# Softmax denominators of an audio-tower block: reciprocals on VectorE in place of a logarithm and an exponential on ScalarE

## The chip, the cores and the metric

The kernel runs on one core of one Trainium2 chip. The metric is the device time of one execution in microseconds (us); lower is better. The kernel before was run three times: 326.23, 329.70 and 332.12 us, median 329.7 us.

## What is computed

The input x has shape (8, 256, 128), float32. Three layers follow one another:

```python
h = tok(x)                      # gated recurrence, (8, 257, 128)
h = h + attn(layernorm(h))      # 8 heads of 16 features
h = h + ffn(layernorm(h))       # shared expert + 16 experts, top 2
```

The layer that matters here is the attention, cut to its core:

```python
scores = einsum('bnhd,bmhd->bhnm', q, k) / sqrt(128)
prob = softmax(scores, axis=-1)
out = einsum('bhnm,bmhd->bndh', prob, v)
```

Keys and values of batch row b come from the other half of the batch (row b+4 or b-4). The feed-forward layer computes all 16 experts and the shared one for every position and weighs them with the router's top two.

## The kernel before, in words

**Units.** The batch is worked off in four units u = 0 to 3 of two rows s = 0, 1 (rows u and u+4, so that each is the other's key and value side). Features lie on the 128 partitions, and the 257 positions, padded to 258 (`W`), lie along the free axis. Each unit passes three stages: T (recurrence, first layer norm, q, k, v), A (attention, second layer norm, routing) and F (13 chunks of 128 feed-forward features, `NF`). The units overlap: while unit u is in F, unit u+1 goes through T and A.

**Order.** A unit's work is cut into pieces with names (`unit_pieces`, L86 to L113), and `ENGINES` (L60) says which engines take part in each: P is TensorE, A ScalarE, V VectorE, G GpSimd, S SyncE. For each engine the table `AT` (L119 to L177) gives every piece of that engine its place; `order` (L195) sorts by it, and `run` (L367) issues the instructions in that order. So each engine works through a fixed list of its own, and semaphores (`S[name]`, waited for with `ge`) tie the lists together. `SLOT` (L180) says which of the four PSUM slots each use of PSUM takes.

**The end of a softmax.** For every (u, s) the product of the exponentiated scores and the values arrives in a PSUM slot ("pv"). The values carry columns of ones, so that numerators and denominators stand in the same slot, in alternating groups of 16 partitions. Then:

- `apart` (L639, ScalarE) copies one bank of the slot, masked, into `rden` (denominators, L645) and `nom` (numerators, L646), both 128x258.
- `join` (L806, VectorE) adds the other bank's half to `rden` (L810) and `nom` (L812), and gives the PSUM slot free.
- `rden_` (L648, ScalarE) takes the natural logarithm of `rden` (L651) and then the exponential of its negative (L653). Ahead of them stands `tables(SET_EXP_LN)`.
- `norm` (L814, VectorE) shuffles the reciprocals onto the numerators' partitions (`swapped`, L817), multiplies (L820) and adds `h1`, the output of the recurrence, into `h2n` (L822).

When both `norm` pieces of a unit are done, TensorE starts the second layer norm (`center`, L1009), whose result feeds the router and the experts. GpSimd's `h1` of the next unit (L474) also waits for the unit before's `h2n`. On ScalarE `keep` (L675) copies `h2n` to `h2`, which the feed-forward sums are added to.

**Tables.** `tables(number)` (L523) issues an activation table load (L527) only when the set differs from the one loaded last in ScalarE's list. Set 6 has the exponential and the logarithm; set 0 has the exponential and tanh. `variance`, `rden_` and pieces 1, 2 and 7 of `token` ask for set 6; `tanh` (L695), once for each of the 13 chunks of a unit, asks for set 0. The exponentials of the scores (`st_`, L627) ask for none.

**Feed-forward.** Chunk c of unit u: TensorE computes the gate and up halves (`half_`, L1145), ScalarE evicts the gate (L686), GpSimd clips it (L499), ScalarE takes tanh (L699), VectorE clips the up half (`clip_up`, L890), combines (`gated`, L896, and `gu`, L911), GpSimd multiplies by the routing weight (L510), TensorE applies the second weight in three bursts (`down`), which VectorE adds (`add`, L914).

Of the kernel before, what the change touches and what calls it, by code (L numbers as in the profile page):

```python
# [25 lines left out]
SET_EXP_LN = 6  # L26
# [10 lines left out]
for _name, _n in (("wtok", 3 * P), ("btok", 3), ("cmat", P), ("omat", P), ("wq", P), ("wk", P), ("wv", P),  # L37
# [48 lines left out]
def unit_pieces(u):  # L86
# [11 lines left out]
    for s in range(2):  # L98
        parts = [(c, i) for c in range(2) for i in range(2)]
        a += [("A", "scores", u, s, *x) for x in parts] + [("A", "max", u, s, *x, h) for x in parts for h in range(2)]  # L100
        a += [("A", n, u, s) for n in ("mlast", "mtop", "plast")]
        a += [("A", "keys", u, s, *x) for x in parts] + [("A", "st", u, s, *x, h) for x in parts for h in range(2)]
        a += [("A", "pvl", u, s)]
        a += [("A", "pv", u, s, c) for c in range(2)] + [("A", n, u, s) for n in ("apart", "join", "rden", "norm")]
# [3 lines left out]
    for c in range(NF):  # L108
# [25 lines left out]
    ),  # L134
# [13 lines left out]
    ),  # L148
# [15 lines left out]
    ),  # L164
# [6 lines left out]
    ),  # L171
    "S": (
        0, 3, 4, 5, 6, 7, 8, 9, 10, 11, 13, 12, 14, 15, 16, 31, 1, 17, 18, 20, 19, 21, 22, 23, 25, 24, 28, 29, 27, 26,
        30, 41, 2, 32, 33, 36, 35, 34, 37, 38, 39, 40, 42, 43, 45, 44, 46, 55, 47, 48, 49, 50, 51, 52, 53, 54, 57, 56,
        59, 58, 61, 60, 62,
# [57 lines left out]
def build(nc, x_in, consts_in, w1_in, w2_in, spill, out):  # L233
    ctx = ExitStack()
    with ctx:
# [282 lines left out]
        def _(act):  # L518
# [129 lines left out]
            def rden_(st, u, s):  # L648
                tables(SET_EXP_LN)
                ge(act, "join", 2 * u + s + 1)  # L650
                a(rden[:, :], rden[:, :], ACT.Ln).then_inc(S["lden"], 1)  # L651
                ge(act, "lden", 2 * u + s + 1)
                a(rden[:, :], rden[:, :], ACT.Exp, scale=-1.0).then_inc(S["rden"], 1)  # L653
# [607 lines left out]
```

## Time and profile before

| | us |
|---|---|
| three runs | 326.23, 329.70, 332.12 (median 329.7) |
| the profiled execution's own time | 330.53 |
| span of the profiled execution, first to last instruction | 328.8 |
| mean granted clock of TensorE, as a share of full speed | 0.957 |

The profiled execution took 330.53 us, of which 1.7 us lie outside the span. Windows and start times in the rows count from the start of the span. "Busy" is time in which an engine executes instructions; waits are not in it.

### The profile page before, as it was taken

Reading aid. Unit: us, or ns where it says so; the run is one execution under the profiler, and the core shown is the slowest. Engines: PE = TensorE matmul, PEld = TensorE weight load, DVE = VectorE, ACT = ScalarE, POOL = GpSimd, SP = SyncE. Lnnn points to the kernel's source line nnn. Section 1 sums busy time; section 2 is a strip of 40 time slices with the busy share of each in tenths; the row PEclk is TensorE's granted clock in tenths of the full one; section 3 lists DMA queues with packets and bytes.
Section 4 is the critical chain, followed back from the end, with each engine's and each line's share of the span. In section 5 each row is a group of like instructions: output and inputs, shape, how many; then the busy total and the mean of one; then the engine's idle time right before and its main releaser. Section 6 shows DMA issues by size and latency. Waiting matters only on the chain.

```text
span 328.8 us, 6060 instructions
## 1 busy us (share of the span) xinstructions
PE 292.7 (89%) x2056; PEld 225.7 (69%) x2056; DVE 261.1 (79%) x488; ACT 237.4 (72%) x406; POOL 159.2 (48%) x138
## 2 busy tenths in 40 slices
PE   7467899968899999999989999999999979997973
PEld 5236665446587777876847968979778769986751
DVE  2397693425999999998899989788989789998870
ACT  3978905859689878799989989777877855754121
POOL 2002830010827857552856864711485643487960
PEclk9879999989999999999999999999999999999585
DMA  6500100000004304100131204100432200064211
GB/s 248 209 8 0 35 1 2 2 0 32 0 6 146 111 5 102 37 2 0 53 89 60 67 0 128 35 9 8 163 104 61 89 7 8 21 179 133 64 40 32
DMA packets 11318, 18.87 MB, mean 57 GB/s; under 512 B 1868, under 2 KB 4052, under 8 KB 11160
## 3 DMA queue, kind: packets, MB, share of 16 engines
q1 hardware_dynamic: 11288, 18.49, 18.1%
q8 instruction: 17, 0.28, 0.3%
q14 instruction: 13, 0.11, 0.1%
HBM read 17.03 MB, written 1.19 MB: 55 GB/s over the span
## 4 chain that ended last, share of the span: by engine, by line
PE 55%; DVE 17%; ACT 13%; issue 7%; POOL 3%; DMA 2%; POOLq 1%; SPq 0%; ACTq 0%; DVEq 0%
PE slot L988 54%; DVE mx L792 3%; DVE ubuf L890 2%; ACT L527 2%; DVE tbuf L911 1%; DMA cst<-in_consts 1%; ACT zabs L539 1%; ACT pt L637 1%; ACT soft L540 1%; DVE h2n L822 1%; DMA cwb<-spill 1%; POOL te L510 1%; PE slot L1186 1%; POOL soft L448 1%; ACT zlog L546 1%
## 5 line engine op out<-in xcount | busy, mean ns | idle before, releaser
L510 POOL TENSOR_TENSOR te<-tbuf,cwb 128x516 f32<-128x516 f32 x48 | 70.9, 1486 | 36.3 <-DVE tbuf L911 31.6
L988 PE MATMUL slot<-xh,w1h 128*128 128x258 f32 x208 | 65.2, 314 | 3.4 <-ACT gbuf L686 0.7
L499 POOL TENSOR_SCALAR gbuf<-gbuf,fpar 128x516 f32<-128x516 f32 x52 | 48.4, 934 | 38.5 <-ACT gbuf L686 38.2
L988 PE MATMUL slot<-xh,w1l 128*128 128x258 f32 x208 | 58.7, 282 | 0.0
L988 PE MATMUL slot<-xl,w1h 128*128 128x258 f32 x208 | 58.7, 282 | 0.0
L988 PE MATMUL slot<-te,w 128*128 128x258 f32 x208 | 52.8, 409 | 4.6 <-POOL te L510 2.4
L988 PEld LDWEIGHTS slot<-te,w 128*128 128x128 f32 x208 | 41.8, 205 | 12.7 <-POOL te L510 3.2
L896 DVE SCALAR_TENSOR_TENSOR tbuf<-tbuf,gbuf 128x516 f32<-128x516 f32 x52 | 46.8, 907 | 3.9 <-ACT tbuf L699 3.8
L988 PEld LDWEIGHTS slot<-xh,w1h 128*128 128x128 f32 x208 | 39.3, 189 | 13.6 <-issue 12.5
L686 ACT ACTIVATE gbuf<-slot,cst 128x516 f32<-128x516 f32 x52 | 35.1, 688 | 18.3 <-PE slot L988 14.8
L699 ACT ACTIVATE tbuf<-gbuf,fpar 128x516 f32<-128x516 f32 x52 | 36.9, 723 | 11.7 <-POOL gbuf L499 8.0
L792 DVE TENSOR_REDUCE mx<-slot 128x2 f32<-128x514 f32 x64 | 40.9, 685 | 2.6 <-PE slot L988 2.4
L890 DVE TENSOR_SCALAR ubuf<-slot,fpar 128x516 f32<-128x516 f32 x48 | 38.2, 806 | 5.5 <-PE slot L988 5.4
L911 DVE SCALAR_TENSOR_TENSOR tbuf<-ubuf,fpar,tbuf 128x516 f32<-128x516 f32 x48 | 39.6, 838 | 0.5
L988 PEld LDWEIGHTS slot<-xl,w1h 128*128 128x128 f32 x208 | 39.5, 190 | 0.6 <-issue 0.2
L637 ACT ACTIVATE pt<-slot 128x516 f32<-128x516 f32 x64 | 34.7, 602 | 7.1 <-PE slot L988 6.8
L988 PEld LDWEIGHTS slot<-xh,w1l 128*128 128x128 f32 x208 | 39.2, 189 | 0.0
L448 POOL TENSOR_TENSOR soft<-soft,zlog 128x1024 f32<-128x1024 f32 x3 | 7.1, 2356 | 48.0 <-ACT zlog L546 48.0
L988 PE MATMUL slot<-ka,qa 32*128 32x258 f32 x256 | 27.1, 425 | 3.1 <-DVE mx L792 1.3
L527 ACT ACT_TABLE_LOAD x22 | 28.2, 1283 | 1.1 <-PEq L1253 0.7
L988 PE MATMUL slot<-qa,ka 32*128 32x258 f32 x256 | 24.8, 420 | 1.2 <-DVE qa L804 0.5
L988 PEld LDWEIGHTS slot<-ka,qa 32*128 32x128 f32 x256 | 14.5, 183 | 11.2 <-DVE mx L792 3.7
(155 smaller groups left out, 482.5 us busy)
## 6 DMA issues: line engine op xcount, KB each, us to landing
cwb<-spill SPq DMA_DIRECT2D x32, 193.5 KB, 2.9
cwb<-spill SPq DMA_DIRECT2D x32, 129.0 KB, 3.0
cwb<-spill SPq DMA_DIRECT2D x32, 64.5 KB, 2.8
pt<-in_w SPq DMA_DIRECT2D x1, 1664.0 KB, 9.0
xt<-in_x SPq DMA_DIRECT2D x4, 256.0 KB, 3.8
out<-osb SPq DMA_DIRECT2D x8, 128.0 KB
w<-in_w SPq DMA_DIRECT2D x1, 832.0 KB, 10.5
cst<-in_consts SPq DMA_DIRECT2D x1, 528.5 KB, 5.4
```

The source lines that it names most:

```text
L448: e.tensor_tensor(soft[:, :, :, :], soft[:, :, :, :], zlog[:, 0:2, :, :], ALU.add).then_inc(S["sp"], 1)
L499: g.tensor_scalar(gbuf[:, p, :, :], gbuf[:, p, :, :], fpar[:, GHI, c:c + 1], fpar[:, GLO, c:c + 1], ALU.min, ALU.max).then_inc(S["gclip"], 1)
L510: g.tensor_tensor(te[:, c % NTE, :, :], tbuf[:, c % NB, :, :], cwb[:, c % NSP, :, :], ALU.mult)\
L527: nc.scalar.add_instruction(mybir.InstLoadActFuncSet(name=nc.get_next_instruction_name(), act_func_set_id=number, ins=[], outs=[]))
L637: release(a(pt[:, c, 4 * h + i:4 * h + i + 3:2, :], scores, ACT.Exp, scale=SCORE_SCALE), st, name)
L686: release(a(gbuf[:, c % NB, :, :], slot(st, ("g", c))[:, :, 0:W], ACT.Identity, bias=par[:, B1G, c:c + 1]), st, ("g", c))
L699: a(tbuf[:, c % NB, :, :], gbuf[:, c % NB, :, :], ACT.Tanh, scale=fpar[:, HA, c:c + 1])\
L792: release(v.tensor_reduce(tops, slot(st, name)[:, :, 0:N], AX_X, ALU.max), st, name)
L890: release(v.tensor_scalar(ubuf[:, p, :, :], slot(st, ("u", c))[:, :, 0:W], hi, lo, ALU.min, ALU.max), st, ("u", c))
L896: v.scalar_tensor_tensor(tbuf[:, p, :, :], tbuf[:, p, :, :], 1.0, gbuf[:, p, :, :], ALU.add, ALU.mult)\
L911: v.scalar_tensor_tensor(tbuf[:, p, :, :], ubuf[:, p, :, :], fpar[:, UB, c:c + 1], tbuf[:, p, :, :], ALU.add, ALU.mult).then_inc(S["gu"], 1)
L988: return nc.tensor.matmul(out_, lhsT, rhs, start=start, stop=stop, **k)
```

## The change

- The piece `rden` is gone from the piece lists, from `ENGINES` and from ScalarE's table of functions, with its table request, its logarithm, its exponential and the semaphore `lden`.
- `norm` on VectorE now waits for `join` itself and issues `v.reciprocal` on `rden` in place, 128x258 float32. The shuffle waits for it.
- `norm` has one more wait, for `h2` at u, ahead of the addition that writes `h2n`: in the kernel before, the copy `keep` of the unit before stood ahead of `rden_` in ScalarE's list, which ordered the two.
- All places in `AT` for the five engines, and the slots in `SLOT`, are new. They hold the same pieces otherwise. The lists differ from those of before mostly by swaps of neighbours and moves over a few places.

```diff
@@ ENGINES, unit_pieces
-    "apart": "A", "join": "V", "rden": "A", "norm": "V", "gate": "PV", ...
+    "apart": "A", "join": "V", "norm": "V", "gate": "PV", ...
-        a += [...] + [("A", n, u, s) for n in ("apart", "join", "rden", "norm")]
+        a += [...] + [("A", n, u, s) for n in ("apart", "join", "norm")]
@@ ScalarE
-            def rden_(st, u, s):
-                tables(SET_EXP_LN)
-                ge(act, "join", 2 * u + s + 1)
-                a(rden[:, :], rden[:, :], ACT.Ln).then_inc(S["lden"], 1)
-                ge(act, "lden", 2 * u + s + 1)
-                a(rden[:, :], rden[:, :], ACT.Exp, scale=-1.0).then_inc(S["rden"], 1)
@@ VectorE
             def norm(st, u, s):
                 n = 2 * u + s + 1
+                ge(dve, "join", n)
+                v.reciprocal(rden[:, :], rden[:, :]).then_inc(S["rden"], 1)
                 ge(dve, "rden", n)
                 v.stream_shuffle(swapped[:, :], rden[:, :], ...).then_inc(S["swap"], 1)
                 released(dve, st, ("pv", s))
                 ge(dve, "swap", n)
                 v.tensor_tensor(nom[:, :], nom[:, :], swapped[:, :], ALU.mult).then_inc(S["even"], 1)
                 ge(dve, "even", n)
+                ge(dve, "h2", u)
                 v.tensor_tensor(h2n[:, s, 0:N], nom[:, 0:N], h1[:, s, 0:N], ALU.add).then_inc(S["h2n"], 1)
```

What the new lists hold around the change, read off the tables of the diff: ScalarE's list asks for a table load 14 times, the first included, where the old one asks 22 times. Of the copies `keep`, that of unit 0 now stands ahead of `apart` of (1, 0); that of unit 1 stands behind it: after `apart` of (2, 0) come one gate eviction, one tanh, two score exponentials, one tanh, and then `keep` of unit 1. In VectorE's list `norm` of (2, 0) follows `join` of (2, 0) with one `clip_up` between them, and `gated` of chunk 4 comes behind it.

## Rows read from the trace of the kernel before

**Rows 1.** The page, busy time, share of the span and instruction counts by engine.

```profile
PE 292.7 (89%) x2056; PEld 225.7 (69%) x2056; DVE 261.1 (79%) x488; ACT 237.4 (72%) x406; POOL 159.2 (48%) x138
```

**Rows 2.** The page, the chain that ended last, shares of the span by engine.

```profile
PE 55%; DVE 17%; ACT 13%; issue 7%; POOL 3%; DMA 2%; POOLq 1%; SPq 0%; ACTq 0%; DVEq 0%
```

**Rows 3.** Busy time by stretch: window, its length, then the engines.

```profile
core 0: us, PE busy (x) PEld busy (x) DVE busy (x) ACT busy (x) POOL busy (x), PEclk, DMA share, GB/s
58.00:70.00 12.00, 10.58 (x90) 5.44 (x82) 5.53 (x14) 7.86 (x18) 1.27 (x1) 1.00 0.00 1
80.00:100.00 20.00, 18.31 (x139) 14.02 (x138) 19.66 (x45) 15.47 (x28) 9.21 (x8) 1.00 0.03 9
100.00:120.00 20.00, 19.59 (x166) 15.12 (x164) 19.27 (x33) 17.04 (x30) 16.51 (x14) 1.00 0.34 101
...
140.00:160.00 20.00, 19.36 (x126) 14.48 (x126) 17.48 (x44) 19.72 (x33) 9.19 (x8) 1.00 0.01 1
160.00:180.00 20.00, 18.48 (x169) 13.24 (x168) 19.96 (x34) 18.31 (x29) 13.36 (x12) 1.00 0.26 76
...
260.00:268.00 8.00, 6.46 (x65) 5.00 (x54) 7.18 (x14) 5.09 (x9) 3.24 (x4) 1.00 0.20 66
...
80.00:180.00 100.00, 95.30 (x735) 72.20 (x733) 95.03 (x179) 87.14 (x143) 60.61 (x49) 1.00 0.17 49
180.00:260.00 80.00, 78.71 (x613) 64.64 (x609) 68.47 (x131) 64.97 (x116) 45.45 (x39) 1.00 0.22 64
```

**Rows 4.** Groups of ScalarE by form: count, busy us, mean ns, idle before.

```profile
L699 ACT ACTIVATE tbuf<-gbuf,fpar 128x516 f32<-128x516 f32 x52 | 36.9, 723 | 11.7 <-POOL gbuf L499 8.0 <-POOL te L510 3.2 <-DVE te L907 0.3
...
L637 ACT ACTIVATE pt<-slot 128x516 f32<-128x516 f32 x64 | 34.7, 602 | 7.1 <-PE slot L988 6.8
L527 ACT ACT_TABLE_LOAD x22 | 28.2, 1283 | 1.1 <-PEq L1253 0.7
```

**Rows 5.** The tile rden: count, ns min/median/max, first and last start.

```profile
L651 ACT ACTIVATE rden<-rden x8: 418/420/468, 61.1 to 263.8; 128x258 f32<-128x258 f32 x8
L653 ACT ACTIVATE rden<-rden x8: 418/419/421, 61.6 to 264.2; 128x258 f32<-128x258 f32 x8
...
L817 DVE STREAM_SHUFFLE swapped<-rden x8: 437/444/452, 62.0 to 264.7; 128x258 f32<-128x258 f32 x8
```

**Rows 6.** The tile gm of the router, VectorE operations on 5 elements a partition.

```profile
L859 DVE TENSOR_TENSOR gm<-gm x4: 153/155/158, 82.2 to 277.8; 128x5 f32<-128x5 f32 x4
...
L866 DVE TENSOR_SCALAR gm<-gm x4: 158/165/1954, 83.4 to 279.0; 128x5 f32<-128x5 f32 x4
L868 DVE RECIPROCAL gm<-gm x4: 189/190/190, 85.4 to 279.1; 128x5 f32<-128x5 f32 x4
```

**Rows 7.** Timeline of VectorE, 58 to 70 us: start, us, what, idle before.

```profile
65.62 0.48 DVE L810 SCALAR_TENSOR_TENSOR rden<-slot,cst,rden 128x258 f32<-128x258 f32 x1 [2.15 <-ACT nom L646]
...
67.04 0.44 DVE L817 STREAM_SHUFFLE swapped<-rden 128x258 f32<-128x258 f32 x1
```

**Rows 8.** The chain that ended last, 110 to 116 us: start, us, what.

```profile
111.97 0.44 DVE swapped L817
```

**Rows 9.** Timeline of VectorE, 127 to 134 us.

```profile
129.07 0.47 DVE L810 SCALAR_TENSOR_TENSOR rden<-slot,cst,rden 128x258 f32<-128x258 f32 x1
...
129.86 0.80 DVE L890 TENSOR_SCALAR ubuf<-slot,fpar 128x516 f32<-128x516 f32 x1
131.13 0.01 DVE L817 LOAD_MASK_SELECT swapped<-rden  x1 [0.47 <-ACT rden L653]
```

**Rows 10.** Timeline of ScalarE, 127 to 134 us.

```profile
128.93 1.28 ACT L527 ACT_TABLE_LOAD   x1
130.22 0.42 ACT L651 ACTIVATE rden<-rden 128x258 f32<-128x258 f32 x1
```

**Rows 11.** Timeline of VectorE, 260 to 268 us.

```profile
262.49 0.48 DVE L810 SCALAR_TENSOR_TENSOR rden<-slot,cst,rden 128x258 f32<-128x258 f32 x1
...
264.68 0.01 DVE L817 LOAD_MASK_SELECT swapped<-rden  x1 [0.59 <-ACT rden L653]
```

More of the change, by code:

```diff
@@ L103, in unit_pieces @@
         a += [("A", "pvl", u, s)]
-        a += [("A", "pv", u, s, c) for c in range(2)] + [("A", n, u, s) for n in ("apart", "join", "rden", "norm")]
+        a += [("A", "pv", u, s, c) for c in range(2)] + [("A", n, u, s) for n in ("apart", "join", "norm")]
     a += [("A", n, u, 2) for n in ("center", "variance", "scale")] + [("A", "gate", u)]
@@ L120 @@
     "P": (
[13 rows of a table removed]
[13 rows of a table added]
     ),
     "A": (
[12 rows of a table removed]
[12 rows of a table added]
     ),
     "V": (
[14 rows of a table removed]
[14 rows of a table added]
     ),
     "G": (
[5 rows of a table removed]
[5 rows of a table added]
     ),
     "S": (
-        0, 3, 4, 5, 6, 7, 8, 9, 10, 11, 13, 12, 14, 15, 16, 31, 1, 17, 18, 20, 19, 21, 22, 23, 25, 24, 28, 29, 27, 26,
-        30, 41, 2, 32, 33, 36, 35, 34, 37, 38, 39, 40, 42, 43, 45, 44, 46, 55, 47, 48, 49, 50, 51, 52, 53, 54, 57, 56,
-        59, 58, 61, 60, 62,
+        0, 3, 4, 5, 7, 6, 10, 9, 8, 11, 12, 15, 13, 14, 16, 31, 1, 17, 18, 19, 20, 21, 22, 23, 24, 25, 27, 29, 26, 28,
+        30, 34, 2, 32, 33, 36, 38, 35, 37, 39, 40, 41, 42, 43, 45, 44, 46, 54, 47, 48, 49, 51, 50, 52, 53, 55, 56, 57,
+        58, 59, 60, 61, 62,
     ),
@@ L330, in build @@
                  "efin h1 sq1 sq2 rs1 rs2 vpad bq bk nm "
-                 "mxl pv apart join swap even lden rden h2n h2 xh xl cwl gtop gexp gclip uclip th gg gu shared te").split()
+                 "mxl pv apart join swap even rden h2n h2 xh xl cwl gtop gexp gclip uclip th gg gu shared te").split()
         S = {n: sem("r_" + n) for n in names}
@@ L727, in _ @@
             run("A", {"token": token, "center": center, "variance": variance, "q": q_, "k": k_, "v": v_, "weights": weights,
-                      "clamps": clamps, "plast": plast, "st": st_, "apart": apart, "rden": rden_, "split": split, "route": route,
+                      "clamps": clamps, "plast": plast, "st": st_, "apart": apart, "split": split, "route": route,
                       "cwt": cwt_, "keep": keep, "g": gate_half, "u": up_half, "tanh": tanh, "out": out_})
```

110 rows, old and new, of tables (AT, ENGINES, SLOT) are left out of this document.

## Prediction

> **What bounds the kernel now.** I read the page's busy times first. TensorE is busy for 292.7 of 328.8 us, VectorE for 261.1, ScalarE for 237.4, GpSimd for 159.2 [rows 1]. The chain of work that ended last gives 55% to TensorE, 17% to VectorE and 13% to ScalarE [rows 2]. So no engine holds the end alone, and the change takes work from the third engine and gives it to the second. What that is worth depends on the stretch, so the windows come next [rows 3]. Three kinds of stretch are to be seen there. From 58 to 70 us, at the end of unit 0's attention, no feed-forward work exists yet that could cover a late softmax: TensorE has 1.4 us of idle time in it, and VectorE and ScalarE have room. From 80 to 180 us TensorE (95.3 of 100) and VectorE (95.0 of 100) are both full, and in two of its windows one engine has nothing left: VectorE 19.96 of 20 from 160 to 180, ScalarE 19.72 of 20 from 140 to 160. From 180 to 260 us TensorE alone is full (78.7 of 80) and VectorE has 11.5 us to spare. Then, from 260 to 268, the last softmax of the last unit opens a hole of 1.5 us in TensorE.
>
> **What ScalarE loses.** Eight logarithms and eight exponentials at 0.42 us [rows 5]: 16 x 0.42 = 6.7 us. Table loads: the new list asks 14 times instead of 22, and one load takes 1.283 us [rows 4]: 8 x 1.283 = 10.3 us. Together 17.0 us of ScalarE's 237.4.
>
> The first activation behind a load starts 0.01 us after it: load at 128.93 for 1.28, logarithm at 130.22 [rows 10]. So I count a load at its own duration. The Trainium skill, in ScalarE: Activation LUTs, section "What ACT_TABLE_LOAD costs", adds a drain of about 1.38 us to the same 1283 ns for every switch, and by it the eight loads would be worth 21.3 us. The trace shows the 1283 ns and no such drain between the load and the next activation. That page's rule is not used in the sum.
>
> **What VectorE gains.** Eight reciprocals on 128x258 float32. The trace of before has no reciprocal of that length, so it is bounded. The only one it has, on 5 elements a partition, takes 190 ns; a two-input operation of the same 5 elements takes 155 ns, a one-input one 165 [rows 6]. Either the difference is fixed for an instruction. Then a long reciprocal is a shuffle of 258 elements (0.444 us [rows 5]) plus 0.03, 0.47 us: the low end. Or it comes with each element. Then it is 35/5 = 7 ns an element against the first row and 25/5 = 5 ns against the second, and the long one takes 0.44 + 258 x 0.005 = 1.73 us or 0.44 + 258 x 0.007 = 2.25 us, the high end. The ends are far apart. I take R = 2.0 us, between the two per-element readings: a fixed surcharge would be odd for an operation whose short form is already dearer than a two-input one. Eight of them add 16.0 us to VectorE (3.8 at the low end, 18 at the high).
>
> The Trainium skill, in VectorE: DVE Perf Modes, section "First, the fixed hardware budget", says that the reciprocal is an iterated divide on the first two slices with a repeat count of 8. If this means eight cycles an element at the 0.96 GHz of the same page, an estimate from it is 258 x 8 / 0.96 = 2.15 us and a little over. It speaks against the change, and it would raise the sum below by some 0.6 us.
>
> **The path through one softmax.** On the path stand `apart`, `join`, the reciprocal and `norm`. Before, the shuffle starts 1.42 us after `join` where no load comes between (65.62 to 67.04 [rows 7]), 2.06 us after it in unit 1 (129.07 to 131.13 [rows 9]) and 2.19 us after it in unit 3 (262.49 to 264.68 [rows 11]), both with a load whose beginning lies under `join`. Afterwards VectorE's next instruction can start 0.79 us after `join` begins (129.07 to 129.86 [rows 9]: the second half of `join`, for the numerators, goes first), then R, then about 0.1 us for its own semaphore. That is 0.89 + 2.0 = 2.9 us.
>
> **The sum.**
> - Unit 0, s = 1: 2.9 - 1.42 = +1.45 us. Nothing covers it, since TensorE waits for this softmax.
> - Unit 1, s = 0: the shuffle lies on the chain as one in a row of VectorE's own instructions [rows 8], in a stretch where VectorE is busy 19.27 of 20 us. R comes in front of all that is queued behind it. TensorE is as full there (19.59), so I take +1.5 of 2.0 us.
> - Unit 1, s = 1: 2.9 - 2.06 = +0.8 at most, TensorE has other work; +0.5.
> - Unit 2, s = 0, and what the stretch of 160 to 180 us pushes on: between 0 and 2.0 us; VectorE has 11.5 us to spare from 180 on, so +0.5.
> - Unit 2, s = 1, and unit 3, s = 0: in 180 to 260 us TensorE is full and VectorE is not; 0. That holds for gains as well as for losses.
> - Unit 3, s = 1: 2.9 - 2.19 = +0.7, exposed, since TensorE has its hole there.
> - The rest of ScalarE's relief. Three loads on the softmax path are already in the differences above; five, 6.4 us, are left, and they and the earlier activations shorten queues that hold TensorE and VectorE in part of the time only. The ends are 0 and -6.4; I take half, -3.2.
> - The new wait for `h2` in `norm`. Only (2, 0) can feel it. ScalarE passes a gate eviction, two tanh, two score exponentials and the copy before it is met: six instructions of 0.6 to 0.72 us [rows 4], 4.0 us after `apart`. VectorE gets there after 0.79 (`join`), 0.73 (one `clip_up`), 2.0, and 0.9 (shuffle and product), 4.4 us. 0, hidden by the reciprocal itself. With R = 0.47 it would be a stall of 1.1 us with `gated` of chunk 4 and all of VectorE's list behind it.
> - The new order of all lists and slots: the same work with moves of a few places. I can't price it piece by piece and take 0, with 4 us to either side.
>
> Sum: 1.45 + 1.5 + 0.5 + 0.5 + 0.7 - 3.2 = +1.45 us. On the profiled execution's 330.53 us this gives 332.0. That execution lies 0.8 us above the median of 329.7, so against the median it is 331.2. I predict 331 us.
>
> **Rivals.**
> - *The reciprocal costs its instruction and little more (R = 0.47).* For it: no row here shows a long one. Against it: the 35 ns on 5 elements. The path from `join` to the shuffle would be 1.36 us: -0.05 in unit 0, -0.7 in unit 1, -0.8 in unit 3; unit 1, s = 0 +0.35; the stall at (2, 0) +1.1, half covered, +0.5; relief -3.2. Sum -3.9, on the median 326 us. Chance 0.22.
> - *ScalarE's relief counts in full and the new lists use it.* The kernel has 36 us in which TensorE is idle, and ScalarE holds 13% of the chain. If half of the 17.0 us comes back, with R at the low end, the sum is -8.5 and the -1 of the path: 320 us. For it: the stretch of 140 to 160 us, where ScalarE is full. Against it: two of the engines are full in the middle whatever ScalarE does. Chance 0.16.
> - *VectorE becomes the engine that sets the pace from 80 to 180 us.* It has 5.0 us left in that stretch, and the reciprocals of unit 1 and the first of unit 2 put 3 x 2.25 = 6.75 us in. The point from which it decides is where VectorE's busy share of that stretch goes past some 98%: everything behind a reciprocal in VectorE's list then moves by its full length, and with it the PSUM slots it frees and GpSimd's multiplications. Price: 6.75, plus 1.7 and 0.95 on the exposed paths of units 0 and 3 at R = 2.25: +9.4 with no relief, 339 us. For it: VectorE's windows at 19.66, 19.27 and 19.96 of 20. Against it: the new lists can move VectorE's work past the reciprocal, and later it has room. Chance 0.20.
>
> **How the numbers follow.** The forecast has a chance of 0.42 and lies between 327 and 335 by its own unknowns (R from 1.73 to 2.25, relief from 0 to -6.4, the order). Going out to the rivals until about 2 in 10 are left out gives 322 to 337. A change of 2% is 6.6 us, about what a measurement of this kernel can tell from none, for its three runs alone differ by 5.9 us; so faster means under 323.1 and slower over 336.3. Faster: nearly all of the second rival and a few hundredths of the first, 0.19. Slower: most of the third and the edge of the forecast, 0.19. Within 2%: 0.62.
>
> **What would show it.** The reciprocal's row: about 2.0 us each; near 0.5 the first rival holds, and over 2.25 the third gains. ScalarE: 14 table loads, busy time near 220 us. VectorE: busy near 277 us. From `join` to the shuffle: about 2.9 us in units 0, 1 and 3. In the windows, VectorE between 80 and 180 us at 97 to 98 of 100 by my forecast, and over 98 with a later end of that stretch by the third rival. The step of unit 0 is right if the second layer norm of unit 0 starts some 1.5 us later against its `apart` than before. The wait at (2, 0) shows as idle time of VectorE in front of L822's successor; I expect none. The prediction is wrong if the time leaves 322 to 337 us, or if it holds while the table loads turn out to have stood on the chain in more places than three.

## The result, and the profile after

The changed kernel took 332.1, 332.2, 333.0 and 334.6 us (median 332.6). Four runs of the kernel before in the same comparison gave 326.2 to 334.3 us (median 330.9). The medians differ by only 1.7 us, because they mix executions in the chip's fast state with executions in a second, slower one; the ratio compares fast ones alone. It is 1.0137, 95% interval 1.0089 to 1.0185: some 4.5 us slower, and less than 2%. The profiled execution of the changed kernel took 332.1 us, its span is 330.3.

The page of the changed kernel, busy time by engine, against [rows 1]:

```profile
PE 292.2 (88%) x2056; PEld 224.4 (68%) x2056; DVE 275.9 (84%) x496; ACT 221.7 (67%) x382; POOL 160.1 (48%) x138
```

VectorE has 14.8 us more and eight instructions more, ScalarE 15.7 us less and 24 instructions less, TensorE the same work. The reciprocal's row in the tile rden of the changed kernel (count, ns min/median/max, first and last start), against [rows 5, 6]:

```profile
L810 DVE RECIPROCAL rden<-rden x8: 1755/1756/1758, 62.0 to 267.5; 128x258 f32<-128x258 f32 x8
```

There are 14 table loads (L527) of 1283 ns each, against 22 [rows 4].

The long reciprocal takes 1.756 us, whatever else runs: eight times within 3 ns. With the short one of 190 ns [rows 6] this makes (1756 - 190) / 253 = 6.2 ns an element.

The timeline of VectorE in the changed kernel, 127 to 134 us, against [rows 9] (start, us, what, idle before):

```profile
130.06 0.49 DVE L803 SCALAR_TENSOR_TENSOR rden<-slot,cst,rden 128x258 f32<-128x258 f32 x1 [0.18 <-ACT nom L646]
...
130.85 1.76 DVE L810 RECIPROCAL rden<-rden 128x258 f32<-128x258 f32 x1
...
132.65 0.44 DVE L812 STREAM_SHUFFLE swapped<-rden 128x258 f32<-128x258 f32 x1
```

`join` to shuffle is 2.59 us here; it was 2.06. It is 2.60 in unit 0 (66.86 to 69.46; before 1.42) and 2.60 in unit 3 (266.69 to 269.29; before 2.19). The wait for `h2` at (2, 0) shows no idle time: the shuffle starts at 186.55, the product at 187.10, the addition at 187.56, as closely as everywhere.

The windows, against [rows 3]:

```profile
core 0: us, PE busy (x) PEld busy (x) DVE busy (x) ACT busy (x) POOL busy (x), PEclk, DMA share, GB/s
80.00:180.00 100.00, 95.14 (x704) 72.61 (x703) 95.06 (x181) 83.30 (x137) 61.76 (x49) 1.00 0.17 51
180.00:260.00 80.00, 77.55 (x608) 62.47 (x607) 73.52 (x132) 53.85 (x101) 40.54 (x37) 1.00 0.23 65
260.00:330.30 70.30, 56.79 (x368) 47.58 (x366) 60.15 (x90) 33.98 (x61) 43.36 (x33) 0.97 0.22 64
```

Of VectorE's 14.8 us more, 3.6 stand ahead of 80 us, about the length of unit 0's two reciprocals. From 80 to 180 us VectorE is as busy as before (95.06 against 95.03). The rest turns up after 180 us, where it had room, 5 us up to 260 and 6 behind. Where the time went can be read from the start of `apart` (L645): (0, 0) at 58.9 before and 60.3 after, (0, 1) at 64.7 and 66.0, (1, 0) at 109.1 and 110.3, (2, 0) at 180.6 and 182.4, (3, 0) at 241.3 and 244.8, (3, 1) at 261.6 and 265.8. So 4.2 us are lost up to the last softmax. 1.4 of them are lost ahead of the first `apart`, before any reciprocal has run, so only the new lists or the clock can be their cause. The two profiles then differ by only 1.5 us at the end. This is because the profiled execution of the kernel before had a low clock in its last stretch:

```profile
300.00:328.80 28.80, 18.15 (x68) 13.78 (x67) 17.14 (x19) 6.79 (x13) 16.02 (x12) 0.69 0.18 56
```

The granted clock there was 0.69, in the changed kernel 0.93 (300 to 330.3 us). The ratio is the better measure, and it agrees with the 4.2 us.

### The profile page after: what moved, and what is told of

Read it like the earlier page. It is cut to its first block and busy times, and to the rows that moved or that the text cites. A ratio compares the mean times of both kernels' runs of the same rounds, so it can differ in the third digit from the quotient of the medians.

```text
span 330.3 us, 6050 instructions
## 1 busy us (share of the span) xinstructions
PE 292.2 (88%) x2056; PEld 224.4 (68%) x2056; DVE 275.9 (84%) x496; ACT 221.7 (67%) x382; POOL 160.1 (48%) x138
## 5 line engine op out<-in xcount | busy, mean ns | idle before, releaser
L510 POOL TENSOR_TENSOR te<-tbuf,cwb 128x516 f32<-128x516 f32 x48 | 71.9, 1506 | 41.1 <-DVE tbuf L907 38.0
L499 POOL TENSOR_SCALAR gbuf<-gbuf,fpar 128x516 f32<-128x516 f32 x52 | 48.8, 943 | 34.3 <-ACT gbuf L679 34.2
L984 PE MATMUL slot<-te,w 128*128 128x258 f32 x208 | 50.0, 393 | 3.2 <-DVE ubuf L886 1.7
L907 DVE SCALAR_TENSOR_TENSOR tbuf<-ubuf,fpar,tbuf 128x516 f32<-128x516 f32 x48 | 47.0, 994 | 0.7
L984 PEld LDWEIGHTS slot<-te,w 128*128 128x128 f32 x208 | 39.7, 195 | 10.8 <-POOL te L510 2.6
L892 DVE SCALAR_TENSOR_TENSOR tbuf<-tbuf,gbuf 128x516 f32<-128x516 f32 x52 | 41.3, 802 | 3.1 <-ACT tbuf L692 3.1
L886 DVE TENSOR_SCALAR ubuf<-slot,fpar 128x516 f32<-128x516 f32 x48 | 38.1, 808 | 2.8 <-PE slot L984 2.6
L984 PE MATMUL slot<-qa,ka 32*128 32x258 f32 x256 | 25.6, 424 | 2.3 <-DVE qa L797 1.4
L984 PEld LDWEIGHTS slot<-ka,qa 32*128 32x128 f32 x256 | 13.9, 183 | 11.6 <-DVE mx L785 2.6
L984 PEld LDWEIGHTS slot<-qa,ka 32*128 32x128 f32 x256 | 13.1, 183 | 11.6 <-issue 5.9
```

The source lines that it names most:

```text
L499: g.tensor_scalar(gbuf[:, p, :, :], gbuf[:, p, :, :], fpar[:, GHI, c:c + 1], fpar[:, GLO, c:c + 1], ALU.min, ALU.max).then_inc(S["gclip"], 1)
L510: g.tensor_tensor(te[:, c % NTE, :, :], tbuf[:, c % NB, :, :], cwb[:, c % NSP, :, :], ALU.mult)\
L886: release(v.tensor_scalar(ubuf[:, p, :, :], slot(st, ("u", c))[:, :, 0:W], hi, lo, ALU.min, ALU.max), st, ("u", c))
L892: v.scalar_tensor_tensor(tbuf[:, p, :, :], tbuf[:, p, :, :], 1.0, gbuf[:, p, :, :], ALU.add, ALU.mult)\
L907: v.scalar_tensor_tensor(tbuf[:, p, :, :], ubuf[:, p, :, :], fpar[:, UB, c:c + 1], tbuf[:, p, :, :], ALU.add, ALU.mult).then_inc(S["gu"], 1)
L984: return nc.tensor.matmul(out_, lhsT, rhs, start=start, stop=stop, **k)
```

## The experiments

Theory A is the prediction's: R lies on the path of each softmax and in front of VectorE's queue, exposed in some places and covered in others. Theory B: the new lists cost. Theory C: VectorE sets the pace everywhere. Theory D was made after run 4: a longer block on VectorE opens a gap in TensorE, the granted clock falls behind the gap, and more is lost than the block. All ratios are to runs of the kernel before on the same chip. Runs 1 to 8 were made on one chip and runs 9 to 12 on another, so their times must not be compared directly (for the first comparison, above, the record names no chip).

What can be compared is the length of a stage inside each profiled execution. This table has them, from the starts of the first `apart` of each unit (us). The numbers in front are those of the experiments. Run 7 is left out, being twice as long, and so is run 1, whose profiled execution took 345.8 us where its fastest took 337.1.

| kernel | start to (0, 0) | (0, 0) to (1, 0) | (1, 0) to (2, 0) | (2, 0) to (3, 0) | (3, 0) to end |
|---|---|---|---|---|---|
| before | 58.9 | 50.2 | 71.5 | 60.7 | 87.4 |
| changed | 60.3 | 50.0 | 72.0 | 62.5 | 85.5 |
| 2: new lists, logarithm | 60.2 | 48.8 | 72.2 | 66.7 | 89.2 |
| 3: cheap operation | 60.3 | 48.0 | 72.0 | 61.5 | 85.3 |
| 4: twice, all units | 60.8 | 53.7 | 79.2 | 69.2 | 92.3 |
| 5: before, no loads | 58.3 | 56.0 | 70.9 | 60.2 | 83.3 |
| 6: unit 0 on ScalarE | 64.0 | 48.1 | 71.1 | 62.1 | 87.1 |
| 8: ahead of numerators | 61.5 | 52.7 | 71.0 | 66.1 | 88.4 |
| 9: twice in unit 0 | 61.4 | 53.1 | 71.1 | 62.4 | 85.8 |
| 10: twice in unit 1 | 61.1 | 49.9 | 79.4 | 62.4 | 85.4 |
| 11: twice in unit 2 | 60.6 | 50.0 | 72.0 | 69.2 | 85.9 |
| 12: twice in unit 3 | 60.2 | 50.0 | 72.0 | 62.4 | 91.9 |

The granted clock is 1.00 in the third and fourth number of a row, except 0.96 where the reciprocals of unit 1 are doubled, 0.95 where those of unit 2 are, and 0.97 from (2, 0) to (3, 0) in runs 2 and 8. Behind (3, 1), in the last column, it lies between 0.87 (before) and 1.00 (run 10), so a difference there is less sure.

**1. Old lists, reciprocal on VectorE.**

```diff
# before.py, AT and SLOT as they were, the piece rden taken out of ScalarE's list
-                a(rden[:, :], rden[:, :], ACT.Ln) ... ACT.Exp
+                v.reciprocal(rden[:, :], rden[:, :]).then_inc(S["rden"], 1)
...
+                ge(dve, "h2", u)
```

> The lists and slots of the kernel before, with the reciprocal on VectorE and ScalarE's logarithm, exponential and eight table loads gone. Theory A (the reciprocal's 1.76 us on the path of each softmax and in front of VectorE's queue is the cost, ScalarE's relief gives part of it back): unit 0 +1.2, unit 1 +1.3 and +0.5, unit 2 +0.4, unit 3 +0.4, relief -2 to -3, so +1 to +3 us against the kernel before, ratio 1.003 to 1.01. Theory B (the new lists are what costs, the reciprocal is neutral or a gain): the ratio is 1.00 or less. In unit 0 the shuffle should start 2.6 us after join under both.

Ratio 1.0279 (1.0202 to 1.0356). Theory A's +1 to +3 us is too little: it is 9 us. Theory B, which wanted 1.00 or less, falls with it: the new lists make the same arithmetic faster, not slower. Which of the moved pieces do that was not tested. VectorE never waits for `h2` in this kernel's trace, so the added wait is not the cause.

**2. New lists, logarithm and exponential on ScalarE.**

```diff
# after.py, the piece rden back in ScalarE's list, directly or three pieces behind apart
+                tables(SET_EXP_LN)
+                a(rden[:, :], rden[:, :], ACT.Ln) ... ACT.Exp
-                v.reciprocal(rden[:, :], rden[:, :]).then_inc(S["rden"], 1)
```

> The new lists and slots with logarithm and exponential put back on ScalarE behind each apart, and the table requests with them. Theory A: the new lists themselves are near neutral, but they were not laid out for these loads, so 0 to +3 us against the kernel before, ratio 1.00 to 1.01. Theory B (the new lists are what costs): the excess of the changed kernel stays or grows, ratio 1.013 or more. Common to both: apart of unit 0 comes about 1.3 us later than in the kernel before, since no reciprocal lies ahead of it.

Ratio 1.0289 (1.0226 to 1.0352), with 24 table loads in lists laid out for 14. Theory A had at most 1.01 and missed; theory B's 1.013 or more came true here, as it had not in run 1. `apart` of (0, 1) starts at 65.9 us, as in the changed kernel. With the first experiment this is a table of four: old lists with logarithm 1.000 and with reciprocal 1.028; new lists with logarithm 1.029 and with reciprocal 1.014. So neither part is slow or fast by itself.

The fourth cell needs care, for the places of the eight `rden` pieces in this run were set by hand. Up to (2, 0) the kernel is level with the other two: `apart` starts at 181.2 us, against 180.6 before and 182.4 in the changed kernel. The next stage is 4.2 us longer than in the changed kernel, and one wait lies in it:

```profile
189.02 0.43 DVE L824 TENSOR_TENSOR h2n<-nom,h 128x257 f32<-128x257 f32 x1 [3.82 <-ACT h L680]
```

VectorE stands still for 3.82 us, for the copy of `h2` that stands behind `apart` of (2, 0) in the new ScalarE list and now has two table loads, a logarithm and an exponential in front of it. Most of the rest, 3.7 us, is in the last stage, where the granted clock behind (3, 1) was lower too (0.92 against 0.97). So 1.029 is an upper end, and nearly half of its 9 us is one badly placed wait.

**3. A cheap operation in place of the reciprocal.**

```diff
-                v.reciprocal(rden[:, :], rden[:, :]).then_inc(S["rden"], 1)
+                v.tensor_tensor(rden[:, :], rden[:, :], rden[:, :], ALU.max).then_inc(S["rden"], 1)
```

> The changed kernel with the reciprocal replaced by an elementwise maximum of the tile with itself, so the division by the denominators is left out; about 0.44 us instead of 1.76. Theory A (only the exposed softmaxes and part of the full stretch count): 1.3 us less at unit 0, some 1 us less at each of unit 1's two and at the last one, together -3 to -5 us against the changed kernel, ratio to the kernel before 0.998 to 1.005. Theory C (VectorE sets the pace, each of its instructions counts): 8 x 1.3 = -10.6 us, ratio near 0.98. Theory B: no change, 1.013.

Ratio 1.0048 (1.0000 to 1.0095). The operation's row:

```profile
L810 DVE TENSOR_TENSOR rden<-rden x8: 418/519/1455, 61.9 to 264.4; 128x258 f32<-128x258 f32 x8
```

It was less cheap than meant: 0.70 us on average, 1.46 in (1, 0) and 1.13 in (3, 0), in both of which GpSimd was working under it. The eight operations are 8.5 us shorter than the eight reciprocals, and VectorE's whole busy time falls by 6.4 us (275.9 to 269.5). The span is 327.1 us against 330.3: -3.2 us, half of the 6.4. This is theory A's figure, in other places than theory A had it. By stages it is -2.0 in unit 0, 0.0 in unit 1, -1.0 in unit 2 and -0.2 from (3, 0) on. In (1, 1) the operation is 1.14 us shorter than the reciprocal and in (3, 1) 1.34 us, and neither shows in the length of its stage. That refutes theory C. In (1, 0) this run tests next to nothing. VectorE also waits 0.4 us for `h2` at (2, 0); the first rival of the prediction, with a short reciprocal, had 1.1.

**4. The reciprocal twice.**

```diff
                 v.reciprocal(rden[:, :], rden[:, :]).then_inc(S["rden"], 1)
+                ge(dve, "rden", 2 * n - 1)
+                v.reciprocal(rden[:, :], rden[:, :]).then_inc(S["rden"], 1)
```

> The changed kernel with the reciprocal issued twice, one behind the other, so the denominators come back as they were and the division is left out; 1.76 + 0.1 us more in each softmax. Theory A: about 3.5 of the 8 count in full, +6 us against the changed kernel, ratio to the kernel before 1.03. Theory C: at least 6 of 8 count, +11 us or more, 1.045. Theory B: +1 us or less.

Ratio 1.0861 (1.0799 to 1.0923), span 355.1: +24.8 us. VectorE is busy for 289.8 us, 13.9 more than in the changed kernel. No theory had said this. Taking 6.4 us of VectorE's work away gives back 3.2; adding 13.9 costs 24.8, 1.8 us for each. TensorE's busy time grew from 292.2 to 302.7 us for the same 2056 matmuls, and its idle time from 38.1 to 52.4. Runs 9 to 12 find where.

**5. The kernel before without the eight loads.**

```diff
-                tables(SET_EXP_LN)
                 ge(act, "join", 2 * u + s + 1)
-                a(rden[:, :], rden[:, :], ACT.Ln).then_inc(S["lden"], 1)
+                a(rden[:, :], rden[:, :], ACT.Identity).then_inc(S["lden"], 1)
```

> The kernel before with rden_ asking for no table: its logarithm is replaced by a plain copy and the exponential runs in whichever set is loaded, so the reciprocals are left out and eight table loads go (22 to 14), with every list as it was. It prices ScalarE's relief alone, with nothing added to VectorE. By my prediction's terms: three loads on the softmax path in stretches of which one and a half are exposed (-2 us) and half of the other five (-3.2 us): -5 us, ratio 0.985. If the relief in full came back: -10 us, 0.97. If loads are hidden in the order made for them: 0 to -2 us, 0.995 or more.

Ratio 1.012 (1.0088 to 1.0152), though ScalarE had 9.9 us less work (227.5 us busy). The prediction's terms wanted 0.985. By all executions the two are closer: four of this kernel took 329.0 to 330.4 us (median 329.4), the eight of the kernel before 325.4 to 335.6 (median 331.0). The stages show both what went wrong and what the loads are worth. The stage from (0, 0) to (1, 0) is 5.8 us longer than in the kernel before, at a granted clock of 0.82 against 0.97:

```profile
80.00:100.00 20.00, 18.61 (x107) 14.82 (x107) 15.40 (x38) 10.68 (x18) 8.40 (x7) 0.73 0.00 1
```

The granted clock is 0.73 from 80 to 100 us, where the kernel before had 1.00 [rows 3]. TensorE is busy for 6.1 us more in this stage (50.3 against 44.3) with the same 337 matmuls. All eight loads that are gone lie later, so they have no part in this loss.

From `apart` of (1, 0) to `apart` of (3, 1) the granted clock is 1.00 in both kernels, and all eight loads that are gone lie there (17 in the kernel before, 9 here):

```profile
114.24:265.64 151.40, 147.72 (x1137) 117.40 (x1138) 136.69 (x253) 118.93 (x209) 89.85 (x75) 1.00 0.20 56
```

That is 151.4 us against 152.5. Eight loads, 10.3 us of ScalarE, are worth 1.1 us in the old lists. What the new lists make of them was not tested. Behind (3, 1) this kernel is another 4.1 us faster, but there the profile of the kernel before has its low clock (0.87 against 0.95).

**6. Unit 0 on ScalarE.**

```diff
-                v.reciprocal(rden[:, :], rden[:, :]).then_inc(S["rden"], 1)
+                if u:
+                    ge(dve, "join", n)
+                    v.reciprocal(rden[:, :], rden[:, :]).then_inc(S["rden"], 1)
# ScalarE: Ln and Exp for u == 0
```

> The changed kernel, but unit 0's two softmaxes take the logarithm and exponential on ScalarE, where set 6 is still loaded, so no table load is added (14 stay). Unit 0's path from join to shuffle goes back from 2.60 to about 1.42 us. If the exposed path of unit 0 counts in full, 1.2 us less than the changed kernel, ratio to the kernel before near 1.010 (the changed kernel had 1.0137). If the lists behind it absorb it, as the near-nothing of a cheap reciprocal suggests for later softmaxes: no change.

Ratio 1.0139 (1.0091 to 1.0187), the changed kernel's 1.0137. The 1.2 us of unit 0 can't be seen in it, since 1.2 us are 0.4% and the interval reaches 0.5% to either side. The stages show them: from (0, 0) to (1, 0) it is 48.1 us against 50.0, as with the cheap operation (48.0). The second layer norm of unit 0 starts 4.02 us after `apart` of (0, 1), against 5.06 in the changed kernel. As a whole the profiled execution is 2.1 us longer than the changed kernel's, for it was already 3.7 us late at its first `apart`.

**7. The reciprocal on GpSimd.**

```diff
-                v.reciprocal(rden[:, :], rden[:, :]).then_inc(S["rden"], 1)
+                g.tensor_tensor(rden[:, :], rden[:, :], minus[:, :].to_broadcast([P, W]), ALU.pow)
```

> The changed kernel with the reciprocal moved to GpSimd, as a power with exponent -1 on the same 128x258 tile, placed in GpSimd's list behind the multiplication that VectorE's list has just fed. Same result as the reference. GpSimd is half idle, so if the power costs it under 2 us, VectorE loses 8 x 1.76 us and the time falls to that of the cheap replacement or under, ratio 1.00 to 1.005. If the power costs several us, every softmax path is that much longer and the whole is slower by 3 to 4 times the excess.

Ratio 2.0462 (2.0414 to 2.0510). The tile rden of this kernel:

```profile
L518 POOL TENSOR_TENSOR rden<-rden,minus x8: 41497/41506/41520, 61.7 to 559.6; 128x258 f32<-128x258 f32 x8
```

One power takes 41.5 us, so GpSimd is no way out with this operation. 8 x 41.5 = 332 us is nearly all of the 335 us lost.

**8. The reciprocal ahead of the numerators.**

```diff
# in join, between the two scalar_tensor_tensor
+                ge(dve, "join", 2 * u + s + 1)
+                v.reciprocal(rden[:, :], rden[:, :]).then_inc(S["rden"], 1)
# and taken out of norm
```

> The changed kernel with the reciprocal issued inside join, ahead of the numerators' half. The path from join's start to the shuffle loses nothing (the numerators' half comes behind the reciprocal and before the shuffle), but the PSUM slot is released 1.76 us later in each softmax, and in the pieces where VectorE's list had other work between join and norm (units 1 to 3, s = 0) the reciprocal now stands ahead of that work. If PSUM slots are what a long instruction holds up: +3 us or more against the changed kernel, ratio 1.02 or more. If only VectorE's own queue counts: within 1 us of it, 1.01 to 1.016.

Ratio 1.0516 (1.0378 to 1.0654). The same instructions, but the PSUM slot comes free 1.76 us later. The longest of TensorE's waits in this kernel (what waited, for what: total, times, longest):

```profile
PE slot L984 <- DVE nom L807: 7.7, 6, 1.5
```

TensorE waits 7.7 us for the slots that the numerators' half frees; the changed kernel has no such row among its waits. In the changed kernel the reciprocal stands behind this release. The place is worth 9.5 us by the spans and some 12 by the ratios, whose interval leaves 8 to 17. Not all of it need be the slot: in units 1 to 3, s = 0, the reciprocal now also stands ahead of the other work between `join` and `norm`, and VectorE waits 1.2 us for `h2`. The run doesn't separate these.

**9 to 12. The reciprocal twice in one unit only.**

```diff
+                if u == U:
+                    ge(dve, "rden", n + s)
+                    v.reciprocal(rden[:, :], rden[:, :]).then_inc(S["rden"], 1)
```

> The changed kernel with the reciprocal issued twice in unit 0's two softmaxes only (their division is left out). Theory A (exposed time only): +1.9 to +3.7 us against the changed kernel, ratio to the kernel before 1.02. Theory D (a longer VectorE block opens a gap in TensorE, the granted clock falls behind it, and the loss is more than the block): +4 to +6 us and a lower clock between 60 and 110 us, ratio 1.026 to 1.032.

> The same in unit 1's two softmaxes only. Theory A by the terms of the prediction (0.75 and 0.6 of the added time): +2.5 us, ratio 1.021. Theory D: a gap of about 2.6 us in TensorE behind the first norm, where it waits for the slot that the down-projection's addition on VectorE frees, and matmuls at the lower clock level behind it; together +5 to +8 us, ratio 1.03 to 1.038.

> The same in unit 2 only. Theory A as the prediction had it (TensorE full, VectorE with room from 180 us on, so 0.5 us at most): +0.5 us, ratio 1.015. Theory D: +5 to +7 us, the gap in TensorE again, ratio 1.03 to 1.035.

> The same in unit 3 only. Theory A: the second softmax is exposed in full, the first is not, +1.9 us, ratio 1.019. Theory D: +5 to +7 us, ratio 1.03 to 1.035. If the four single runs sum to about the 24 us of the kernel with two reciprocals everywhere, the costs add; if they sum to much less, it is their crowding that costs.

| unit | ratio (interval) | span, us | more than the changed kernel |
|---|---|---|---|
| 0 | 1.0201 (1.0103 to 1.0299) | 333.9 | 3.6 |
| 1 | 1.0293 (1.0194 to 1.0392) | 338.2 | 7.9 |
| 2 | 1.0224 (1.0128 to 1.0320) | 337.6 | 7.3 |
| 3 | 1.0252 (1.0131 to 1.0373) | 336.5 | 6.2 |

Each adds 2 x 1.8 = 3.6 us to VectorE. The last column compares executions on two chips, and the ratios less 0.0137 say less: 0.006, 0.016, 0.009 and 0.012, 0.042 in sum against 0.072 in run 4, each uncertain by 0.01. The stages decide. Against the changed kernel, the doubled unit's own stage grows by 3.1, 7.4, 6.7 and 6.4 us, and its other stages behind (0, 0) stay within 0.4 us of the changed kernel's, but for one that is 0.9 shorter. The four together are 23.7 us. In run 4, with all eight doubled on the first chip, the same stages grow by 3.7, 7.2, 6.7 and 6.8, 24.3 us. So the costs add up.

Unit 0 costs its own length, as theory A has it, and not the 4 to 6 us of theory D. Units 1 to 3 cost about twice theirs, unit 2 among them, for which theory A had 0.5 us. That is theory D, though its ratios of 1.030 and more for units 2 and 3 were not reached. Part of the growth is TensorE working more slowly: it is busy for 2.7 us more in the stage of unit 1, and 3.8 more in that of unit 2 (60.96 us in the changed kernel), at granted clocks of 0.96 and 0.95 instead of 1.00. The stage of unit 2, doubled:

```profile
182.54:251.77 69.23, 64.78 (x470) 51.25 (x470) 59.10 (x106) 44.55 (x86) 31.64 (x28) 0.95 0.18 52
```

What it is made of can be seen at the first softmax of unit 1. TensorE of the kernel with unit 1 doubled, timeline from 118 us:

```profile
118.93 0.28 PE L989 MATMUL slot<-xh,w1l 128*128 128x258 f32 x1
121.81 0.36 PE L989 MATMUL slot<-xh,w1h 128*128 128x258 f32 x1 [2.60 <-DVE h L924]
122.01 0.28 PE L989 MATMUL slot<-xl,w1h 128*128 128x258 f32 x1
...
123.28 0.42 PE L989 MATMUL slot<-xl,w1h 128*128 128x258 f32 x1
...
123.71 0.42 PE L989 MATMUL slot<-xh,w1h 128*128 128x258 f32 x1
```

And VectorE of the same kernel:

```profile
113.46 1.75 DVE L810 RECIPROCAL rden<-rden 128x258 f32<-128x258 f32 x1
115.25 1.77 DVE L813 RECIPROCAL rden<-rden 128x258 f32<-128x258 f32 x1
...
117.60 0.82 DVE L820 TENSOR_TENSOR nom<-nom,swapped 128x258 f32<-128x258 f32 x1
118.46 1.39 DVE L823 TENSOR_TENSOR h2n<-nom,h 128x257 f32<-128x257 f32 x1
119.77 1.29 DVE L897 SCALAR_TENSOR_TENSOR tbuf<-tbuf,gbuf 128x516 f32<-128x516 f32 x2
120.99 0.68 DVE L924 TENSOR_TENSOR h<-slot,h 128x516 f32<-128x516 f32 x1
```

TensorE stands still for 2.60 us, for a slot that the down-projection's addition (L924) frees. That addition is in VectorE's list behind the whole `norm`. In the changed kernel it came 5.8 us after `join` (111.40 to 117.16), here 8.9 (112.07 to 120.99): 1.8 us for the second reciprocal, and 1.4 us because the product and the addition behind it took 0.82 and 1.39 us where they had taken 0.43 each. GpSimd was working under both here (117.38 to 119.57) and idle in the changed kernel (114.71 to 116.73); that this is the reason was not tested. 1.1 us after TensorE starts again its matmuls follow each other every 0.21 us instead of every 0.12. The windows from `apart` of (1, 0) to `apart` of (1, 1), first in this kernel:

```profile
110.99:133.97 22.98, 20.04 (x151) 15.32 (x150) 21.71 (x31) 13.84 (x25) 16.46 (x14) 0.93 0.23 59
```

then in the changed kernel:

```profile
110.34:129.18 18.84, 18.84 (x151) 14.13 (x148) 18.43 (x29) 13.69 (x25) 15.05 (x13) 1.00 0.24 72
```

The same 151 matmuls: 4.1 us more, of which 2.9 are idle time of TensorE and 1.2 are longer matmuls at a granted clock of 0.93 instead of 1.00, part of the stretch at 1.2 GHz instead of 2.4. In the changed kernel TensorE has no idle time in this stretch at all. So at this softmax one reciprocal of 1.76 us just fits under what TensorE has queued, and the next microsecond opens a gap, which the clock then enlarges.

## Why the prediction was right

The time lies in the range, within 2%, on the slower side, as forecast: +1.45 us predicted, 4.5 measured (2.9 to 6.1 by the interval). That the sum came this near is luck in part, since it rests on a relief that was not found and on costs put into the wrong stages. Step by step:

- *R.* Predicted 2.0 us, measured 1.756, near the lower per-element reading of 1.73. The reading by elements was right. A fixed surcharge, the first rival, is refuted, and run 3 gives about what that rival would have been worth: 1.0048.
- *Work moved.* 14 loads, ScalarE 221.7 us (220), VectorE 275.9 (277): right.
- *The path.* Predicted 0.89 us + R, measured 0.84 + 1.756 = 2.60 in all three units.
- *Unit 0, exposed.* The second layer norm starts 5.06 us after `apart` of (0, 1), before 3.88: 1.2 us later, which is the predicted 1.45 with R at 1.76. This was the sign given for the step. Doubling its two reciprocals costs 3.1 us of its stage for 3.6 us. That the second is covered by nothing was said; the first, which the sum had left out, counts too once it is doubled (`apart` of (0, 1) comes 6.8 us after that of (0, 0), and 5.6 in the changed kernel).
- *Unit 1, +1.5 and +0.5.* Its stage is 0.5 us longer than before, not 2.0, with what the loads give back already in it. In (1, 1), 1.14 us less changed nothing (run 3); for (1, 0) no run gives the price.
- *Unit 2, and (3, 0): 0.5 and 0.* The stage from (2, 0) to (3, 0) is 1.8 us longer than before, and run 3 gives back 1.0. The reason given, that TensorE is full there and VectorE has room, is what failed. Doubled, unit 2 costs 6.7 us in its own stage. VectorE's average room from 180 us on is of no use to a list in fixed order: the instruction behind the reciprocal frees a slot for which TensorE comes at a given moment. The new lists leave most of the room that the first 1.76 us need; the old ones did not (1.028).
- *Unit 3, s = 1: +0.7, exposed.* From `join` to the shuffle it is +0.4 us (2.60 against 2.19), but the second layer norm starts 5.05 us after `apart` of (3, 1), before 5.11. The addition into `h2n` had taken 0.88 us before and takes 0.43 now. Nothing is left of the 0.7.
- *VectorE at 97 to 98% from 80 to 180 us.* It stayed at 95.06. The third rival, VectorE as pace-maker, did not come about in the changed kernel, and theory C fell with run 3. It does describe what happens beyond the corner, in runs 4 and 10 to 12.
- *ScalarE's relief, -3.2.* This term was mis-sized: eight loads less are worth 1.1 us in run 5, where the clock is full in both kernels, and that includes the three on the softmax path. Without the term the prediction's sum is +4.65 us, and about +3.7 with R at 1.76, near the measured 4.5. But the stages above show that this sum too would be near by errors that cancel.
- *Loads on the chain.* The prediction named more than three places with a table load on the chain as a sign against it. The chain of the kernel before has five loads. Three stand ahead of a softmax's logarithm (128.93, 196.94 and 262.47 us), and those are gone; the two others (140.47 and 150.20) are asked for by the new lists too. So by the letter the sign came, and for the loads that the change removes three was right.
- *The new lists, 0 with 4 us either way.* As a part alone they have no price; together with the reciprocal they are worth 1.0279 - 1.0137, 4.7 us by the midpoints. That they were needed at all for the change to stay near even was not in the prediction.
- *The wait for `h2`.* Hidden, as said, and by the reciprocal itself, as said: with shorter work in its place the wait shows (0.4 us in run 3, 3.8 in run 2).

What stays open: the 1.4 us by which the first `apart` comes later. No reciprocal stands ahead of it, and run 2, which has none at all, shows the same start (60.2). The low clock of the first 60 us (0.88 from 20 to 60 us here, 0.99 before) is not enough either: run 5, with the old lists, reaches its first `apart` at 58.3 us, at a mean granted clock of 0.88 up to there against 0.89 in the changed kernel. What differs is that the new lists put two more scans of the recurrence (`zlog`) ahead of it, and VectorE is busy for 37.9 us up to there instead of 35.7. That this costs the 1.4 us was not tested by itself.

## What to carry to other kernels

Where each engine works through a fixed list, a longer instruction is priced by what stands behind it in that list (which PSUM slot it frees, and when TensorE comes for it), and not by the engine's free time over a stretch. Such a price has a corner: up to it the list absorbs most of the instruction, beyond it TensorE stands still and then runs slower too, and in this kernel a microsecond then cost nearly two. So lay out the order anew when a duration changes, and put the release of a buffer ahead of the long instruction.

## What the runs showed of the hardware

- VectorE's float32 reciprocal costs about 6.2 ns an element (190 ns at 5 elements, 1756 ns at 258), some four times a shuffle of the same tile (446 ns). The Trainium skill, VectorE: DVE Perf Modes, section "First, the fixed hardware budget", gives a repeat count of 8. Eight cycles an element at that page's 0.96 GHz, an estimate, would be 8.3 ns. The trace shows 6.2, so the count is not the number of cycles an element.
- VectorE's two-input maximum on 128x258 float32 took 0.42 us with GpSimd idle, and up to 1.46 with GpSimd working (run 3, (1, 0)). The reciprocal in the same place of the changed kernel, with the same GpSimd instructions under it, took 1.758, like all others.
- GpSimd's power, float32, 128x258: 41.5 us, 161 ns an element.
- A gap of 2.60 us in an otherwise full TensorE was followed, 1.1 us after its end, by matmuls at 0.21 us each instead of 0.12; in the same kernel they are back at 0.12 by 127 us. The granted clock was 0.50 from 122.8 to 126.1 us, that is 1.2 GHz, and 1.00 in the changed kernel's whole stretch.
- The activation behind a table load starts within 0.02 us of the load's end in the changed kernel as before (load at 113.41 for 1.28, tanh at 114.70).
